# Reordering the start and the second attention batch of a two-block adaLN kernel in split fp32r

## The chip, the cores and the metric

The kernel runs on 1 NeuronCore of a Trainium2 chip. The metric is the device time in microseconds (us) of one execution, as the median of three runs. Below, PE is TensorE, DVE is VectorE, ACT is ScalarE, POOL is GpSimd, and SP is the engine whose queue issues all DMAs.

## The reference

Four batches of 512 tokens by 512 features pass through an attention-like block and then a feed-forward block, each with its own adaptive layer norm.

```python
mod = (_silu(c) @ wmod).reshape(4, 6, 1, -1)        # sa, ca, ga, sb, cb, gb
h = _layernorm(x) * (1 + ca) + sa
x = x + ga * attn(h)                                # ga, gb: sign kept, magnitude at least 0.25
h = _layernorm(x) * (1 + cb) + sb
x = x + gb * ffn(h)
...
def attn(X):
    Xn = _layernorm(X, gamma, beta)
    Q, K, V = split(Xn @ W_in + b_in)
    K, V = rotary(K), rotary(V)                     # first half of the features
    A = sum over tokens of (K/|K|) * (V/|V|)        # one row of 512 per batch
    A = 0.5 * A + 0.5
    return (A * Q) @ W_out + b_out + X
def ffn(x):
    top-2 gate, softmax summed; relu(x @ W_up.T) @ W_down.T + sum * (x @ W_expert)
```

## The kernel before, in words

**Arithmetic.** Every fp32 product is made of three fp32r products: each operand is split into a high part (ACT or POOL copies it to fp32r) and a low part (original minus high part, on DVE or POOL), and `three` (L1223) multiplies high by high, high by low and low by high. So each weight chunk of 128 rows needs a high and a low part before PE can use it. `split_hi_kv(i, k)` on ACT (L574) makes the high part of chunk k of W_K (i=0) or W_V (i=1). The low part comes from `low_kv(i, k)` on POOL (L428) or `split_lo_kv(i, k)` on DVE (L1076).

**Order.** There is no scheduler. Each engine's instructions stand in the order in which they are written, and semaphores join the engines. A wait therefore holds up everything behind it on its engine. Attention runs over the batches b = 0 to 3, then the feed-forward block over the same batches.

**The start (batch 0).** SP loads the columns, then four 256 KB chunks of the scale rows (wmod[1], into the slot of x batch 2), row tile 0 of x, four 256 KB chunks of the shift rows (wmod[0], into the slot of x batch 3), row tile 1 of x, the identity, row tiles 2 and 3, and the eight chunks of W_K and W_V in turn. PE multiplies the scale chunks (bank 2) and then the shift chunks (bank 3) in `mod_first` (L1233). For each row tile t of x, DVE takes the row's statistics (`x0_stats`, L1047), subtracts and scales (`scale_row0`, L1058), applies 1/std and the shift (`h_row0`, L1068), and takes statistics of the result. POOL raises to the power -0.5 (`rstd_x0`, `shift_h0`), ACT normalises to z, PE transposes z (`transposes0`), ACT applies gamma and beta and makes the high part (`t0_evac`), and DVE makes the low part (`t0_split`). Only then does PE start `kv_tile(0, 0)`.

**One attention batch b (`attention` on each engine, L344, L683, L973, L472).** PE runs `kv_tile(b, 0)`, the output rows of batch b-1, `kv_tile(b, 1)` to `(b, 3)`, and then four chunks of Q, with the transposes of the next batch's z between them. `transposes(b+1, 0)` waits for all four row tiles of z. `transposes(b+1, 2)` and `kv_tile(b, 3)` wait for `kv_products` on DVE, which reads the PSUM banks that they overwrite (`kv_tile(b, 3)` for those of tile 1, `transposes(b+1, 2)` for those of tile 3). Last come `a_sums`, which wait for DVE's `a_pairs`. DVE adds biases (`kv_rows`), makes rotated products (`kv_products`, L858), sums them with weights from POOL (`kv_sum`), finishes the output rows of batch b-1 (`finish_rows`, after the gates have come from DRAM in batch 1), and builds h of batch b+1: `h_row` (L808) adds the shift to what POOL's `scale_rows` (L463) scaled, and `h_stats`, `h_aggr`, POOL's `rstd_h` and DVE's `h_shift` give ACT what `normalise` needs.

**Statistics of x for the later batches.** Batch 1 takes them at the start, batch 2 between the Q splits of `attention(1)` on DVE. Batch 3 takes them in `attention(1)` too, mostly on ACT: `x_sums` and `x_squares` (L591, L599) are eight passes with accumulation, `x_mean` and `x_var` on DVE (L790, L795) finish them, POOL's `rstd_x(3)` and DVE's `x_shift(3)` follow, and ACT runs `normalise_x(3)` at the very end of `attention(1)`, ahead of `q_evac(1, 0)`.

Of the kernel before, what the change touches and what calls it, by code (L numbers as in the profile page):

```python
# [37 lines left out]
def build(nc, X, cols, ident, rot, w, wmod, brow, out):  # L38
# [14 lines left out]
    with ctx:  # L53
# [49 lines left out]
        xss = sb("xss", [P, NT])  # L103
# [13 lines left out]
        xjunk = sb("xjunk", [P, D], mybir.dt.bfloat16)  # L117
# [64 lines left out]
        xsum_s = sem("xsum_s")  # L182
        xmn_s = sem("xmn_s")
# [102 lines left out]
        def _(sp):  # L286

            sp.dma_start(col[:], cols).then_inc(col_in, 16)
            for k in range(NC):
                sp.dma_start(x_slot(2)[:, k * D:(k + 1) * D], wmod[1][:, k * D:(k + 1) * D]).then_inc(ca_w[k], 16)  # L290
            def load_x0(i):
                rows0 = X0_PARTS[i]
                sp.dma_start(x_slot(0).rearrange("p (t d) -> p t d", t=NT)[:, rows0, :],
                             x_batch[0][:, rows0, :]).then_inc(x0_in[i], 16)

            load_x0(0)
            for k in range(NC):
                sp.dma_start(x_slot(3)[:, k * D:(k + 1) * D], wmod[0][:, k * D:(k + 1) * D]).then_inc(sa_w[k], 16)
# [80 lines left out]
        def _(pool):  # L379
# [92 lines left out]
            def attention(b):  # L472
# [17 lines left out]
                else:  # L490
# [11 lines left out]
                    if b + 2 < B:  # L502
                        rstd_x(b + 2)
# [26 lines left out]
            shift_h0(1)  # L530
            rstd_x0(2)
            low_kv(0, 1)
# [3 lines left out]
            low_kv(1, 3)  # L536
# [13 lines left out]
        def _(act):  # L550
# [39 lines left out]

            def x_sums():  # L591

                act.wait_ge(x_in, (B - 1) * 16)
                for t in range(NT):
                    wait(act, xsum_s, t)
                    nc.scalar.activation(xjunk[:], xs[:, tok(B - 1, t)], ACT.Identity,
                                         accum_out=xsum[:, t:t + 1]).then_inc(xsum_s, 1)

            def x_squares():  # L599

                act.wait_ge(xmn_s, 1)
                for t in range(NT):
                    act.wait_ge(xsum_s, NT + t)
                    nc.scalar.activation(xjunk[:], xs[:, tok(B - 1, t)], ACT.Square, bias=xmn[:, t:t + 1],
                                         accum_out=xss[:, t:t + 1]).then_inc(xsum_s, 1)
# [77 lines left out]
            def attention(b):  # L683
# [20 lines left out]
                if b + 2 < B:  # L704
                    normalise_x(b + 2)
# [10 lines left out]
            split_hi_kv(0, 1)  # L716
            normalise(0, 1, 1)
            split_hi_kv(1, 1)
# [46 lines left out]
        def _(dve):  # L765
# [24 lines left out]
            def x_mean():  # L790

                dve.wait_ge(xsum_s, NT)
                v.tensor_scalar(xmn[:], xsum[:], -1.0 / D, None, ALU.mult).then_inc(xmn_s, 1)

            def x_var():  # L795
                dve.wait_ge(xsum_s, 2 * NT)
                v.tensor_scalar(xve[:], xss[:], 1.0 / D, EPS, ALU.mult, ALU.add).then_inc(xve_s, 1)

            def x_shift(g):
                dve.wait_ge(xrs_s, g + 3)  # L800
                wait(dve, xn_s, (g - 1) * NT)
                if g < B - 1:
                    v.scalar_tensor_tensor(xnm[:], xmv[:, :, 0], -1.0, xrs[:], ALU.mult, ALU.mult).then_inc(xnm_s, 1)
                else:
                    dve.wait_ge(xmn_s, 1)
                    v.tensor_tensor(xnm[:], xmn[:], xrs[:], ALU.mult).then_inc(xnm_s, 1)
# [166 lines left out]
            def attention(b):  # L973
# [16 lines left out]
                if b == 1:  # L990
                    x_mean()
                kv_sum(b, 0)
                if b < B - 1:
                    h_row(b + 1, 0)
                else:
# [23 lines left out]
                if b + 2 < B:  # L1019
                    x_shift(b + 2)  # L1020
# [55 lines left out]
            def split_lo_kv(i, k):  # L1076
                dve.wait_ge(whi_v if i else whi_k, k + 1)
                dve.wait_ge(wlo_v if i else wlo_k, k)
                v.tensor_tensor(w_lo_of(W_ORDER[i], k), w_raw[i][:, k * D:(k + 1) * D],
# [33 lines left out]
            h_row0(3)  # L1113
            t0_split(1)
# [105 lines left out]
        def _(pe):  # L1220
# [12 lines left out]
            def mod_first(bank, src, sems):  # L1233
                for k in range(NC):
                    pe.wait_ge(sems[k], 16)
                    last = mm(ps[:, bank, :], sc0[:, k, :], src[:, k * D:(k + 1) * D], start=(k == 0), stop=(k == NC - 1))
                last.then_inc(bc_ps, 1)
# [138 lines left out]
            mod_first(2, x_slot(2), ca_w)  # L1376
            mod_first(3, x_slot(3), sa_w)
# [118 lines left out]
```

## Time and profile before

| what | value |
|---|---|
| three runs | 363.78 us median (363.32 to 365.0) |
| the profiled execution | 365.14 us, of which the span of the instructions is 363.4 us |
| granted PE clock | 1.00 in every slice of the span |
| PE busy | 353.1 us, 97% of the span |
| DVE, ACT, POOL busy | 247.9, 159.1 and 126.6 us |
| DMA | 27.45 MB, most of it in the first 70 us |

The page's timeline divides the span into 40 slices of 9.1 us. PE is at 90% and more in nearly all of them, and less in the first three. DVE is at 90% and more from the fourth slice to the eighth (27 to 73 us). Idle time of PE counts one for one, since it is busy to the end; the question for any other engine is whether PE waits for it.

A matmul's own duration is modelled as longer than its share of the array: in a run of them, one starts about 0.23 us after the other and shows 0.40 us. So the idle time that is written at a stall of PE is about 0.16 us less than what the stall costs.

### The profile page before, as it was taken

What the parts mean: (1) busy time and instruction counts of PE and PEld (TensorE: products, weight loads), DVE (VectorE), ACT (ScalarE), POOL (GpSimd) and SP (SyncE); (2) the same over time, 40 slices, a digit from 0 to 9 for tenths busy, and PEclk for the clock granted to TensorE, in tenths of its full rate; (3) what the DMA queues carried; (4) which work ended last, traced back from release to release, by engine and by line L of the source; (5) the groups of instructions that cost most, each with busy time, mean ns of one, the idle gap of its engine ahead of it and who ended that gap; (6) DMA issues with size and microseconds to landing.
All of it is one profiled execution on the core that took longest, in us unless ns stands there. A gap on an engine that the chain in (4) does not pass through costs nothing.

```text
span 363.4 us, 4952 instructions
## 1 busy us (share of the span) xinstructions
PE 353.1 (97%) x1794; PEld 288.5 (79%) x1794; DVE 247.9 (68%) x508; ACT 159.1 (44%) x301; POOL 126.6 (35%) x131
## 2 busy tenths in 40 slices
PE   8799999999999999999999999999999999999996
PEld 5257587788777788888888898988988898889885
DVE  2689999979977778786977469338623852382474
ACT  1296838647169501476018753444234423441110
POOL 0395879777726166243531324800100010000000
PEclk9999999999999999999999999999999999999999
DMA  6998482370120000000000003101100110011003
GB/s 182 388 406 317 194 318 89 137 213 0 25 63 2 0 2 29 1 1 2 0 31 0 0 2 115 32 0 58 60 0 2 58 59 2 0 60 58 2 1 115
DMA packets 10985, 27.45 MB, mean 76 GB/s; under 512 B 1216, under 2 KB 1600, under 8 KB 9808
## 3 DMA queue, kind: packets, MB, share of 16 engines
q1 hardware_dynamic: 10960, 27.13, 21.1%
q8 instruction: 14, 0.23, 0.3%
q14 instruction: 11, 0.09, 0.1%
HBM read 22.90 MB, written 4.23 MB: 75 GB/s over the span
## 4 chain that ended last, share of the span: by engine, by line
PE 60%; DVE 12%; ACT 8%; issue 7%; DMA 5%; POOL 5%; SPq 2%; POOLq 0%; DVEq 0%; ACTq 0%
PE ps L1225 19%; PE ps L1227 19%; PE ps L1226 19%; PE ps L1284 2%; DMA gate_bc<-mod_rows 2%; DMA xs<-in_X 2%; POOL w_lo L414 2%; DVE hb L815 1%; DVE hst L825 1%; ACT z L626 1%; POOL hrs L411 1%; ACT ps L638 1%; DMA mod_rows<-xs 1%; ACT ps L585 1%; ACT z L617 1%
## 5 line engine op out<-in xcount | busy, mean ns | idle before, releaser
L1225 PE MATMUL ps<-wv_hi,t_hi 128*128 128x260 f32 (+1 forms) x192 | 61.7, 322 | 0.9 <-POOL wv_lo L414 0.5
L1227 PE MATMUL ps<-wv_hi,t_lo 128*128 128x260 f32 (+1 forms) x192 | 61.4, 320 | 0.0
L1226 PE MATMUL ps<-wv_lo,t_hi 128*128 128x260 f32 (+1 forms) x192 | 61.4, 320 | 0.0
L1225 PE MATMUL ps<-w_hi,g_hi 128*128 128x512 f32 (+1 forms) x132 | 51.2, 388 | 0.0
L1225 PE MATMUL ps<-t_hi,w_hi 128*128 128x512 f32 x128 | 50.6, 396 | 0.1
L1227 PE MATMUL ps<-w_hi,g_lo 128*128 128x512 f32 (+1 forms) x132 | 50.6, 383 | 0.0
L1226 PE MATMUL ps<-w_lo,g_hi 128*128 128x512 f32 (+1 forms) x132 | 50.6, 383 | 0.0
L1227 PE MATMUL ps<-t_hi,w_lo 128*128 128x512 f32 x128 | 50.0, 390 | 0.0
L1226 PE MATMUL ps<-t_lo,w_hi 128*128 128x512 f32 x128 | 49.9, 390 | 0.0
L1225 PEld LDWEIGHTS ps<-wv_hi,t_hi 128*128 128x128 f32 x192 | 36.1, 188 | 5.1 <-POOL wv_lo L414 1.4
L411 POOL TENSOR_TENSOR hrs<-hve,expo 128x4 f32<-128x4 f32 (+2 forms) x12 | 11.1, 923 | 81.9 <-DVE hve L832 62.8
L1227 PEld LDWEIGHTS ps<-wv_hi,t_lo 128*128 128x128 f32 x192 | 36.1, 188 | 2.9
L1226 PEld LDWEIGHTS ps<-wv_lo,t_hi 128*128 128x128 f32 x192 | 36.1, 188 | 2.8
L1225 PEld LDWEIGHTS ps<-w_hi,g_hi 128*128 128x128 f32 x132 | 24.8, 188 | 5.1 <-DVE g_lo L907 0.5
L1227 PEld LDWEIGHTS ps<-w_hi,g_lo 128*128 128x128 f32 x132 | 24.8, 188 | 4.9
L1226 PEld LDWEIGHTS ps<-w_lo,g_hi 128*128 128x128 f32 x132 | 24.8, 188 | 4.7
L1227 PEld LDWEIGHTS ps<-t_hi,w_lo 128*128 128x128 f32 x128 | 24.0, 188 | 5.1
L1225 PEld LDWEIGHTS ps<-t_hi,w_hi 128*128 128x128 f32 x128 | 24.1, 188 | 5.0 <-issue 0.4
L1142 DVE SCALAR_TENSOR_TENSOR g_lo<-ps,g_hi 128x512 fp32r<-128x512 f32 x16 | 11.1, 692 | 24.7 <-ACT g_hi L655 24.6
L1226 PEld LDWEIGHTS ps<-t_lo,w_hi 128*128 128x128 f32 x128 | 24.1, 188 | 4.7
L571 ACT ACTIVATE sqj<-ps 128x512 bf16<-128x512 f32 x16 | 9.5, 591 | 41.5 <-DVE ps L854 36.5
L1225 PE MATMUL ps<-w_hi,t_hi 128*128 128x512 f32 x64 | 26.1, 408 | 1.2 <-DVE prod L873 0.9
(153 smaller groups left out, 703.8 us busy)
## 6 DMA issues: line engine op xcount, KB each, us to landing
stage<-in_w SPq DMA_DIRECT2D x5, 1024.0 KB, 4.8
out<-xs SPq DMA_DIRECT2D x15, 256.0 KB, 2.0
xs<-in_X SPq DMA_DIRECT2D x3, 1024.0 KB, 9.5
xs<-in_wmod SPq DMA_DIRECT2D x8, 256.0 KB, 5.9
stage<-in_w SPq DMA_DIRECT2D x8, 256.0 KB, 8.1
xs<-in_wmod SPq DMA_DIRECT2D x2, 1024.0 KB, 7.7
gate_bc<-mod_rows SPq DMA_DIRECT2D x8, 256.0 KB, 3.9
gate_bc<-in_wmod SPq DMA_DIRECT2D x1, 1024.0 KB, 13.3
```

Source lines behind the costliest of these rows:

```text
L411: nc.gpsimd.tensor_tensor(hrs[:, t0:t0 + n], hve[:, t0:t0 + n], expo[:, 0:n], ALU.pow).then_inc(hrs_s, n)
L414: nc.gpsimd.tensor_tensor(w_lo_of(W_ORDER[i], k), w_raw[i][:, k * D:(k + 1) * D], w_hi_of(W_ORDER[i], k).bitcast(f32), ALU.subtract).then_ ...
L571: nc.scalar.activation(sqj[:], src, ACT.Square, accum_out=nsq[:, t % 2, i:i + 1]).then_inc(nsq_s, 1)
L585: nc.scalar.activation(part, part, ACT.Identity, bias=col[:, COL_BETA + c:COL_BETA + c + 1], scale=col[:, COL_GAMMA + c:COL_GAMMA + c + 1] ...
L617: nc.scalar.activation(z[:, t, :], xs[:, tok(g, t)], ACT.Identity, bias=xnm[:, t:t + 1], scale=xrs[:, t:t + 1]).then_inc(xn_s, 1)
L626: nc.scalar.activation(z[:, t, :], src, ACT.Identity, bias=hnm[:, t:t + 1], scale=hrs[:, t:t + 1]).then_inc(z_s, 1)
L638: nc.scalar.activation(whole, whole, ACT.Identity, bias=bias, scale=scale).then_inc(t_full, 1)
L1142: v.scalar_tensor_tensor(g_lo[:, c, :], ps[:, U_BANKS[c % 2], :], 0.0, g_hi[:, c, :].bitcast(f32), ALU.max, ALU.subtract).then_inc(u_los, 1)
L1225: mm(dst, l_hi, r_hi, start=start, stop=False)
L1226: mm(dst, l_hi, r_lo, start=False, stop=False)
L1227: return mm(dst, l_lo, r_hi, start=False, stop=stop)
L1284: last = nc.tensor.transpose(ps[:, t_bank(g, c), t * P:(t + 1) * P], z[:, t, c * P:(c + 1) * P], idn[:])
```

## The change

It has five parts.

1. SP loads shift chunk 0 right behind scale chunk 0, and row tile 0 of x stays behind the scales. PE multiplies in the order scale 0, shift 0, scale 1 to 3, shift 1 to 3.
2. Weight parts: POOL makes the low part of W_K chunk 1 ahead of `rstd_x0(2)`. The low part of W_V chunk 3 moves from POOL to DVE, between `h_row0(3)` and `t0_split(1)`. ACT makes the high part of W_V chunk 1 ahead of `normalise(0, 1, 1)`.
3. Statistics of x batch 3: the passes on ACT, `x_mean` and `x_var` are gone. DVE takes them with `bn_stats` between the Q splits of `attention(2)`, as batch 2's are taken in `attention(1)`. `rstd_x(3)` moves to the end of POOL's `attention(1)`, and `x_shift(3)` and `normalise_x(3)` move into `attention(2)`.
4. `h_row(b+1, 0)` moves on DVE from ahead of `kv_rows(b, 1)` to behind `kv_products(b, 1)`, in batches 1 and 2.
5. One wait in `split_lo_kv` stands twice.

```diff
             sp.dma_start(col[:], cols).then_inc(col_in, 16)
-            for k in range(NC):
-                sp.dma_start(x_slot(2)[...], wmod[1][...]).then_inc(ca_w[k], 16)
+            load_scale(0)
+            load_shift(0)
+            for k in range(1, NC):
+                load_scale(k)
             load_x0(0)
-            for k in range(NC):
-                sp.dma_start(x_slot(3)[...], wmod[0][...]).then_inc(sa_w[k], 16)
+            for k in range(1, NC):
+                load_shift(k)
             load_x0(1)
...
POOL attention(b):
                     weight(b, 1)
-                    if b + 2 < B:
-                        rstd_x(b + 2)
                     rstd_h(b + 1, 0, NT)
...
                     for t in range(NT):
                         base(b + 1, t)
+                    if b == 1:
+                        rstd_x(3)
...
POOL start:
             shift_h0(1)
+            low_kv(0, 1)
             rstd_x0(2)
-            low_kv(0, 1)
             low_kv(1, 1)
             low_kv(1, 2)
             low_kv(0, 3)
-            low_kv(1, 3)
             shift_h0(2)
...
ACT attention(b):
                 norm_sums(b, 0)
-                if b == 1:
-                    normalise_x(2)
-                    x_sums()
-                    x_squares()
+                if b < B - 1:
+                    normalise_x(b + 1)
                 norm_sums(b, 1)
...
                     t_evac(b + 1, c)
-                if b + 2 < B:
-                    normalise_x(b + 2)
...
ACT start:
             split_hi_kv(0, 1)
+            split_hi_kv(1, 1)
             normalise(0, 1, 1)
-            split_hi_kv(1, 1)
...
DVE attention(b):
                     q_split(b - 1, c)
-                    if b == 1:
-                        x_row_stats(2, c)
-                if b == 1:
-                    x_aggr(2)
+                    if b < B - 1:
+                        x_row_stats(b + 1, c)
+                if b < B - 1:
+                    x_aggr(b + 1)
                 kv_rows(b, 0)
                 kv_products(b, 0)
-                if b == 1:
-                    x_shift(2)
+                if b < B - 1:
+                    x_shift(b + 1)
...
                 finish_rows(b - 1)
-                if b == 1:
-                    x_mean()
                 kv_sum(b, 0)
-                if b < B - 1:
-                    h_row(b + 1, 0)
-                else:
+                if b == B - 1:
...
                 kv_rows(b, 1)
-                if b == 1:
-                    x_var()
                 kv_products(b, 1)
                 if b < B - 1:
+                    h_row(b + 1, 0)
                     h_row(b + 1, 1)
...
                 kv_products(b, 2)
-                if b + 2 < B:
-                    x_shift(b + 2)
                 kv_sum(b, 2)
...
DVE start:
             h_row0(3)
+            split_lo_kv(1, 3)
             t0_split(1)
...
PE start:
-            mod_first(2, x_slot(2), ca_w)
-            mod_first(3, x_slot(3), sa_w)
+            first_rows()
```

On POOL at the start, behind the second small product for the first row tile, the kernel before has this (xrs is 1/std of x's rows, hrs and hnm that of h; w_lo belongs to W_K and wv_lo to W_V):

```order
L398 TENSOR_TENSOR hnm<-xmn,hrs 128x1
L381 TENSOR_TENSOR xrs<-xve,expo 128x2
L414 TENSOR_TENSOR w_lo<-stage,w_hi 128x512
L414 TENSOR_TENSOR wv_lo<-stage,wv_hi 128x512 x2
L414 TENSOR_TENSOR w_lo<-stage,w_hi 128x512
L414 TENSOR_TENSOR wv_lo<-stage,wv_hi 128x512
L411 TENSOR_TENSOR hrs<-hve,expo 128x1
```

and the change has this:

```order
L403 TENSOR_TENSOR hnm<-xmn,hrs 128x1
L419 TENSOR_TENSOR w_lo<-stage,w_hi 128x512
L386 TENSOR_TENSOR xrs<-xve,expo 128x2
L419 TENSOR_TENSOR wv_lo<-stage,wv_hi 128x512 x2
L419 TENSOR_TENSOR w_lo<-stage,w_hi 128x512
L416 TENSOR_TENSOR hrs<-hve,expo 128x1
```

So xrs of row tiles 2 and 3 now stands behind a low part, and one low part is gone.

On DVE in `attention(1)`, from the last output row of batch 0 to the statistics of the next h, the kernel before has this (hb<-hb,sa_bc is `h_row`):

```order
L916 TENSOR_TENSOR hb<-ps,hb 128x512
L793 TENSOR_SCALAR xmn<-xsum 128x4
L882 TENSOR_SCALAR acc<-prod,wgt 128x768
L815 TENSOR_TENSOR hb<-hb,sa_bc 128x512
L854 TENSOR_TENSOR ps<-ps,bkv_bc 128x512
L856 TENSOR_TENSOR v_sb<-ps,bkv_bc 128x512
L797 TENSOR_SCALAR xve<-xss 128x4
L863 TENSOR_TENSOR cross<-ps,v_sb 128x128
...
L873 TENSOR_TENSOR prod<-ps,rot_sb 128x256
L815 TENSOR_TENSOR hb<-hb,sa_bc 128x512
L819 BN_STATS hst<-hb 128x6 x2
```

and the change has this:

```order
L887 TENSOR_TENSOR hb<-ps,hb 128x512
L853 TENSOR_SCALAR acc<-prod,wgt 128x768
L825 TENSOR_TENSOR ps<-ps,bkv_bc 128x512
L827 TENSOR_TENSOR v_sb<-ps,bkv_bc 128x512
L834 TENSOR_TENSOR cross<-ps,v_sb 128x128
...
L844 TENSOR_TENSOR prod<-ps,rot_sb 128x256
L786 TENSOR_TENSOR hb<-hb,sa_bc 128x512 x2
L790 BN_STATS hst<-hb 128x6 x2
```

Three instructions fewer stand ahead of the products of tile 1, and one more (the moved `h_row`) behind them.

## Rows read from the trace of the kernel before

**Rows 1.** The page: busy us (share of the span) and instructions of each engine.
```profile
PE 353.1 (97%) x1794; PEld 288.5 (79%) x1794; DVE 247.9 (68%) x508; ACT 159.1 (44%) x301; POOL 126.6 (35%) x131
```

**Rows 2.** Timeline, PE's stalls in batch 1: start us, us, engine line op [idle before <-releaser].
```profile
94.18 0.48 PE L1225 MATMUL ps<-w_hi,t_hi 128*128 128x512 f32 x1 [0.87 <-DVE prod L873]
...
105.93 1.09 PE L1284 MATMUL ps<-idn,z 128*128 128x128 f32 x8 [0.46 <-ACT z L626]
...
110.33 0.84 PE L1284 MATMUL ps<-idn,z 128*128 128x128 f32 x6 [0.56 <-DVE prod L873]
```

**Rows 3.** Timeline, DVE, the statistics of row tile 1 of x.
```profile
13.17 0.69 DVE L1051 BATCH_NORM_STATS2 xst<-xs 128x6 f32<-128x512 f32 x1 [2.45 <-DMA xs<-in_X]
```

**Rows 4.** Timeline, ACT and POOL, weight parts at the start.
```profile
20.67 0.62 ACT L577 ACTIVATE w_hi<-stage 128x512 fp32r<-128x512 f32 x1
```
```profile
20.56 0.71 POOL L381 TENSOR_TENSOR xrs<-xve,expo 128x2 f32<-128x2 f32 x1
21.36 1.30 POOL L414 TENSOR_TENSOR w_lo<-stage,w_hi 128x512 fp32r<-128x512 f32 x1
22.61 1.31 POOL L414 TENSOR_TENSOR wv_lo<-stage,wv_hi 128x512 fp32r<-128x512 f32 x1
```

**Rows 5.** Timeline, DVE, row tile 2 to the statistics of batch 1.
```profile
22.25 0.75 DVE L1074 SCALAR_TENSOR_TENSOR hb<-hb,xrs,ps 128x512 f32<-128x512 f32 x1
...
24.11 0.68 DVE L1079 TENSOR_TENSOR w_lo<-stage,w_hi 128x512 fp32r<-128x512 f32 x1
...
27.88 2.46 DVE L777 BATCH_NORM_STATS2 xst<-xs 128x6 f32<-128x512 f32 x4
```

**Rows 6.** Timeline, PE: start of the first row tile, W_K chunk 2, second row tile.
```profile
21.55 0.50 PE L1225 MATMUL ps<-w_hi,t_hi 128*128 128x512 f32 x1
...
24.87 0.47 PE L1225 MATMUL ps<-w_hi,t_hi 128*128 128x512 f32 x1
...
29.32 0.39 PE L1225 MATMUL ps<-w_hi,t_hi 128*128 128x512 f32 x1
```

**Rows 7.** Timeline, POOL's row scaling, and one DVE operation beside it and alone.
```profile
35.85 4.57 POOL L470 TENSOR_TENSOR hb<-z,ca_bc 128x512 f32<-128x512 f32 x3
```
```profile
37.49 1.77 DVE L815 TENSOR_TENSOR hb<-hb,sa_bc 128x512 f32<-128x512 f32 x1
...
40.38 0.68 DVE L815 TENSOR_TENSOR hb<-hb,sa_bc 128x512 f32<-128x512 f32 x1
```

**Rows 8.** Timeline, the end of batch 0 on ACT and PE.
```profile
54.77 1.52 ACT L626 ACTIVATE z<-hb,hnm,hrs 128x512 f32<-128x512 f32 x2 [5.65 <-DVE hnm L836]
```
```profile
56.59 1.03 PE L1284 MATMUL ps<-idn,z 128*128 128x128 f32 x8
```

**Rows 9.** Timeline, DVE in batch 1.
```profile
85.35 0.95 DVE L793 TENSOR_SCALAR xmn<-xsum 128x4 f32<-128x4 f32 x1
...
87.86 1.79 DVE L815 TENSOR_TENSOR hb<-hb,sa_bc 128x512 f32<-128x512 f32 x1
...
93.95 1.29 DVE L815 TENSOR_TENSOR hb<-hb,sa_bc 128x512 f32<-128x512 f32 x1
...
99.22 0.17 DVE L832 TENSOR_SCALAR hve<-hmv 128x4 f32<-128x4 f32 x1
```

**Rows 10.** Timeline, POOL in batch 1.
```profile
92.14 2.56 POOL L470 TENSOR_TENSOR hb<-z,ca_bc 128x512 f32<-128x512 f32 x2
```

**Rows 11.** Timeline, PE and DVE about the output rows of batch 1 and in batch 2.
```profile
122.27 0.39 PE L1227 MATMUL ps<-w_hi,g_lo 128*128 128x512 f32 x1
122.71 0.50 PE L1225 MATMUL ps<-w_hi,g_hi 128*128 128x512 f32 x1
```
```profile
137.43 0.70 DVE L854 TENSOR_TENSOR ps<-ps,bkv_bc 128x512 f32<-128x512 f32 x1 [2.57 <-PE ps L1227]
...
141.33 0.42 DVE L873 TENSOR_TENSOR prod<-ps,rot_sb 128x256 f32<-128x256 f32 x1
...
156.85 0.42 DVE L873 TENSOR_TENSOR prod<-ps,rot_sb 128x256 f32<-128x256 f32 x1
```

More of the change, by code:

```diff
@@ L102, in build @@
         nmu = xmn
-        xss = sb("xss", [P, NT])
         xst = sb("xst", [P, NT, 6])
@@ L116, in build @@
         sqj = sb("sqj", [P, D], mybir.dt.bfloat16)
-        xjunk = sb("xjunk", [P, D], mybir.dt.bfloat16)
         a_col = sb("a_col", [P, NC])
@@ L181, in build @@
         base_s = sem("base_s")
-        xsum_s = sem("xsum_s")
-        xmn_s = sem("xmn_s")
         kv_ps, kb_s, kv_sb = sem("kv_ps"), sem("kb_s"), sem("kv_sb")
@@ L288, in _, with load_scale, load_shift @@
             sp.dma_start(col[:], cols).then_inc(col_in, 16)
-            for k in range(NC):
+            def load_scale(k):
                 sp.dma_start(x_slot(2)[:, k * D:(k + 1) * D], wmod[1][:, k * D:(k + 1) * D]).then_inc(ca_w[k], 16)
+            def load_shift(k):
+                sp.dma_start(x_slot(3)[:, k * D:(k + 1) * D], wmod[0][:, k * D:(k + 1) * D]).then_inc(sa_w[k], 16)
             def load_x0(i):
@@ L589, in t0_evac @@
                                      ACT.Copy).then_inc(t_his, 1)
[L591 to L605, printed above, removed]
             def normalise_x1(t):
@@ L788, in x_aggr @@
                 v.tensor_scalar(xve[:], xmv[:, :, 1], EPS, None, ALU.add).then_inc(xve_s, 1)
[L790 to L797, printed above, removed]
             def x_shift(g):
@@ L801, in x_shift @@
                 wait(dve, xn_s, (g - 1) * NT)
-                if g < B - 1:
-                    v.scalar_tensor_tensor(xnm[:], xmv[:, :, 0], -1.0, xrs[:], ALU.mult, ALU.mult).then_inc(xnm_s, 1)
-                else:
-                    dve.wait_ge(xmn_s, 1)
-                    v.tensor_tensor(xnm[:], xmn[:], xrs[:], ALU.mult).then_inc(xnm_s, 1)
+                v.scalar_tensor_tensor(xnm[:], xmv[:, :, 0], -1.0, xrs[:], ALU.mult, ALU.mult).then_inc(xnm_s, 1)
             def h_row(g, t):
@@ L989, in attention @@
                 finish_rows(b - 1)
-                if b == 1:
-                    x_mean()
                 kv_sum(b, 0)
-                if b < B - 1:
-                    h_row(b + 1, 0)
-                else:
+                if b == B - 1:
                     for t in range(NT):
@@ L1078, in split_lo_kv @@
                 dve.wait_ge(wlo_v if i else wlo_k, k)
+                dve.wait_ge(wlo_v if i else wlo_k, k)
                 v.tensor_tensor(w_lo_of(W_ORDER[i], k), w_raw[i][:, k * D:(k + 1) * D],
@@ L1231, in idle_products, with first_scale, first_shift, first_rows @@
                     mm(ps[:, IDLE_BANK, 0:2 * P], acc[:, 0:P], acc[:, 0:2 * P], start=True, stop=True)
[L1233 to L1236, printed above, removed]
+            def first_scale(k):
+                pe.wait_ge(ca_w[k], 16)
+                return mm(ps[:, 2, :], sc0[:, k, :], x_slot(2)[:, k * D:(k + 1) * D], start=(k == 0), stop=(k == NC - 1))
+            def first_shift(k):
+                pe.wait_ge(sa_w[k], 16)
+                return mm(ps[:, 3, :], sc0[:, k, :], x_slot(3)[:, k * D:(k + 1) * D], start=(k == 0), stop=(k == NC - 1))
+            def first_rows():
+                first_scale(0)
+                first_shift(0)
+                for k in range(1, NC):
+                    last = first_scale(k)
+                last.then_inc(bc_ps, 1)
+                for k in range(1, NC):
+                    last = first_shift(k)
                 last.then_inc(bc_ps, 1)
```

1 line of the change is left out of this document (removed).

## The prediction

> **What bounds the kernel now.** I read the page first: PE is busy for 97% of the span [rows 1]. What a change of order can win is therefore only time in which PE waits. I then went through PE's timeline for those places. From 30 us to the end there are three of weight, all in batch 1 [rows 2]: 0.87 us on DVE's products of tile 1, 0.46 us on ACT's z, 0.56 us on DVE's products of tile 3. With the 0.16 us that a modelled end hides they cost 1.03, 0.62 and 0.72 us, 2.4 us together. A fourth is small: the last chunk of the first output row starts 0.44 us after its forerunner instead of 0.23 [rows 11], 0.2 us. Batches 2 and 3 show nothing like it. The start is the other place, since PE's first tile runs from 21.55 us to 29.32 us [rows 6], 7.8 us, although its 24 matmuls are 5.6 us of work at 0.23 us each.
>
> **Shift chunk ahead (part 1).** The bytes in front of row tile 1 of x stay the same, so it lands when it did, at 13.17 us [rows 3]. DVE takes that row's statistics (0.69 us and two short steps) before it applies the shift to row tile 0, and these end at about 14.1 us, when PE's shift product is finished in either order. I take 0 us. What hides the product is that landing and those statistics; without them PE would gain one chunk's product, some 0.4 to 0.9 us. The scale rows end one chunk later, and row tile 0 lands one chunk later; both have a microsecond or more until 13.17 us, since DVE waited 2.45 us there [rows 3].
>
> **Weight parts (part 2).** On POOL the low part of W_K chunk 1 cannot come sooner than before: its high part on ACT ends at 20.67 + 0.62 = 21.29 us, and it started at 21.36 us [rows 4]. So the change buys nothing with its first move, and xrs of row tiles 2 and 3, which filled the gap from 20.56 us, comes behind it: from 22.61 to 23.3 us. DVE's `h_row0(2)` waits for xrs and goes from 22.25 to 23.4 us, +1.15 us [rows 5]. The low part of W_K chunk 2, on DVE, stood 1.86 us behind it (24.11 us) and is now wanted at 25.25 us. There POOL is at work on W_V's chunk 2, and this decides how the move is priced. One and the same addition of two SBUF tensors on DVE took 1.77 us while POOL scaled rows, and 0.68 us alone [rows 7]: it stood still until POOL's instruction was done. By that, DVE gets its turn when POOL's chunk ends (POOL's pace is 22.61 - 21.36 = 1.25 us each, so xrs to 23.3, W_V 1 to 24.6, W_V 2 to 25.9) and ends at about 26.4 us. PE starts chunk 2 at 26.45 us instead of 24.87, +1.6 us [rows 6]. From here it has 12 matmuls to its second tile, 2.8 us, where it needed 4.45 us before because it waited for POOL's last low parts. With W_V chunk 3 on DVE that wait is short, and the second tile begins at about 29.5 us instead of 29.32: **+0.2 us**, between -0.4 (DVE is not held) and +0.6.
>
> The Trainium skill, "SBUF — State Buffer", Shared GPSIMD/Vector port, says that DVE operations with two SBUF inputs and GpSimd operations take a common port pair as an exclusive lock for the whole instruction. The 1.77 us beside 0.68 us agree. Without such a lock the moved low part would be free work on DVE, and this part would be -0.4 us instead of +0.2; the rule speaks against moving it while POOL works, and for counting each `h_row` beside POOL at twice its length or more.
>
> DVE itself comes out later than PE. It has the 1.15 us, 0.6 us for the added low part and some 0.3 us of standing still, less the near 1 us that it idled ahead of its second split: batch 1's statistics start at about 29.2 us instead of 27.88, +1.3 us [rows 5]. From there to the end of batch 0 DVE has hardly a gap (90% and more busy in each slice of the page), so the lateness is carried. PE meets it at `transposes(1, 0)`: z was done at 54.77 + 1.52 = 56.29 us and used at 56.59 us [rows 8], 0.3 us of slack. So batch 0 ends later by 1.3 - 0.3 = **+1.0 us**, which includes the 0.2 above. Bounds: -0.4 us, if POOL's turns swallow DVE's lateness, as a DVE operation that arrives late at a busy POOL loses nothing; +2.2 us, if it is held once more on each of two scalings in [rows 7].
>
> **Batch 1 (parts 3 and 4).** Taken away ahead of DVE's products of tile 1: `x_mean` 0.95 us, and `h_row(2, 0)` 1.79 us [rows 9]. These 2.7 us are more than the 1.03 us of the first stall, so **that stall goes**. The next one is another matter. `transposes(2, 0)` needs z of all rows, z needs the statistics that DVE finished at 99.22 + 0.17 = 99.39 us [rows 9], and the moved `h_row(2, 0)` now stands inside that chain. DVE can start on tile 1 when PE has done it: PE wants tile 3 at 94.18 - 1.03 = 93.15 us, tile 2 ahead of it is 24 matmuls or 5.6 us, so at 87.6 us and a little more, 87.85. Batch 2 needed from 137.43 to 141.33 + 0.42 = 141.75 us, 4.3 us, for that work [rows 11], with one operation held by POOL; without that it is about 3.5 us. So the products are done and the rows of h start at 91.3 to 92.4 us, instead of 93.95 us for the second of them [rows 9]. But POOL is in its two scalings from 92.14 us, 2.56 us [rows 10], so both first rows are held for about a scaling each, where one was held before (1.29 us). The end of the statistics comes to 98.6 us in the better order of turns and 99.7 us in the worse, against 99.39 us. I take the middle, -0.25 us. **So the first stall's 1.03 us largely comes back as a longer second one**, and of 2.4 us I count -0.25, and another -0.15 for `x_shift(3)`, which leaves the chain to the third stall. Bounds: -2.4 (all stalls go) and +0.3.
>
> **Batch 2 (parts 3 and 4).** The 0.2 us ahead of the output rows goes, since `normalise_x(3)` no longer stands ahead of ACT's Q evacuation: **-0.2 us** (0 to -0.2). DVE gets four row statistics between the Q splits; `attention(1)` does the same with batch 2's and PE doesn't wait there. `h_row(3, 0)` now stands behind the products of tile 1. The chain from 137.43 us ended at 156.85 + 0.42 = 157.27 us [rows 11], about 0.2 us before PE wanted it. One more row is 0.6 us, less what POOL, undisturbed by the row, is sooner. I take **+0.1 us**, between 0 and +0.5. Batch 3 and the feed-forward block are untouched.
>
> **Sum.** +1.0 - 0.25 - 0.15 - 0.2 + 0.1 = **+0.5 us**. The profiled execution took 365.14 us for a span of 363.4 us, 1.4 us over the median of the runs; on its own time the sum gives a span of 363.9 us and 365.6 us, on the median 363.78 + 0.5 = **364.3 us**. A measurement of this kernel tells about 0.5%, 1.8 us, from no change.
>
> **The rivals.**
> - *All of batch 1's stalls go and the start breaks even (0.17).* For it: the 2.7 us taken away exceed the 2.4 us of stalls, batch 2 runs the same instructions without them, and the turns of POOL and DVE may fall well. Against it: POOL scales batch 1's rows at 92.14 us, where batch 2's are early. 363.78 - 2.4 - 0.2 + 0.3 = 361.5 us.
> - *DVE's late start of batch 0 compounds (0.18).* Its place is `h_row0(2)`, which waits for xrs behind a low part. If DVE comes to POOL's scalings after 36 us so late that it is held once more, the lateness is 2.2 us or more at `transposes(1, 0)` and PE pays it; it decides from 2.1 us on. With the worse turns in batch 1 (+0.15) and +0.3 in batch 2: 363.78 + 2.2 + 0.15 - 0.2 + 0.3 = 366.2 us, slower.
> - *The start is swallowed (0.15).* PE's slack and POOL's turns absorb DVE's 1.3 us: 363.78 + 0 - 0.4 - 0.1 = 363.3 us.
> - *The reordered loads change when row tile 1 of x lands (0.05).* Everything up to 30 us hangs on 13.17 us, and the trace has one order only. By a chunk or more either way, about 1 us: 363.3 or 365.3 us.
>
> **How the numbers follow.** The forecast, anything within a microsecond of 364.3, has 0.45. The first rival is mostly below 361.96 (0.5% faster), the second mostly above 365.6: **0.17 faster, 0.65 same, 0.18 slower**. The range leaves out the outer half of each of the two: **362.0 to 366.2 us**.
>
> **What would show it.** In the profile after: x's row tile 1 still at about 13.2 us; DVE's row with xrs of tile 2 at about 23.4 us; PE at W_K chunk 2 near 26.4 us and at the second tile near 29.5; `transposes(1, 0)` about 1 us late with PE idle on ACT's z; no idle of PE on products of tile 1 in batch 1, but about 1.3 us ahead of `transposes(2, 0)`, on z; two long `h_row` there; nothing ahead of the output rows of batch 1; a few tenths ahead of `transposes(3, 2)`. I am wrong if PE starts chunk 2 before 25.5 us, if `transposes(1, 0)` is on time, or if the stall on z in batch 1 is gone too.

## The result, and the profile after

The changed kernel takes 365.62 us (median of 20 runs, 364.82 to 366.05), the kernel before beside it 364.46 us (20 runs, 362.38 to 365.32). The ratio is 1.0039, 95% interval 1.0029 to 1.0048: slower by 0.39% by the ratio and by 1.16 us (0.32%) by the medians, a difference that the interval bears out, and within the 0.5% that the prediction calls no change. The forecast was 364.3 us, range 362.0 to 366.2. The kernel before spreads over almost 3 us and the changed one over 1.2 us. That is a finding too: 17 of the changed kernel's 20 runs are slower than the slowest run of the kernel before.

The changed kernel's profiled execution took 364.96 us (span 363.1 us), at the low end of its runs; that of the kernel before took 365.14 us (363.4 us), at the high end of its own. Put side by side, these two profiles say "0.2 us faster".

Busy times on the page after [rows 1]:

```profile
PE 353.1 (97%) x1794; PEld 288.7 (80%) x1794; DVE 249.6 (69%) x516; ACT 153.4 (42%) x285; POOL 124.7 (34%) x130
```

PE's sum is the same. ACT has 16 instructions and 5.7 us less, which are the eight statistics passes and the reads of their sums. DVE has 8 instructions and 1.7 us more.

The statistics of x's row tile 1 started 0.76 us earlier than in the profile before [rows 3]. The six profiles with the old order of loads have this row anywhere from 12.30 to 13.50 us and the eight with the new order from 12.41 to 12.89, so one profile of each says nothing about the order. Everything below is compared by its distance from this row:

```profile
12.41 0.69 DVE L1015 BATCH_NORM_STATS2 xst<-xs 128x6 f32<-128x512 f32 x1 [0.53 <-DMA xs<-in_X]
```

Timeline after, POOL and then DVE, weight parts at the start [rows 4, 5]:

```profile
20.61 1.30 POOL L419 TENSOR_TENSOR w_lo<-stage,w_hi 128x512 fp32r<-128x512 f32 x1 [0.84 <-ACT w_hi L581]
21.86 0.72 POOL L386 TENSOR_TENSOR xrs<-xve,expo 128x2 f32<-128x2 f32 x1
22.53 2.56 POOL L419 TENSOR_TENSOR wv_lo<-stage,wv_hi 128x512 fp32r<-128x512 f32 x2
```
```profile
22.61 0.75 DVE L1038 SCALAR_TENSOR_TENSOR hb<-hb,xrs,ps 128x512 f32<-128x512 f32 x1 [1.22 <-POOL xrs L386]
...
24.47 1.17 DVE L1044 TENSOR_TENSOR w_lo<-stage,w_hi 128x512 fp32r<-128x512 f32 x1
...
28.29 2.46 DVE L761 BATCH_NORM_STATS2 xst<-xs 128x6 f32<-128x512 f32 x4
```

The chain is the one forecast: xrs behind the low part, DVE 1.22 us idle on it, and W_K chunk 2's low part held until POOL's two W_V chunks ended (25.09 us), 1.17 us where it took 0.68.

Timeline after, PE: its stalls over 0.2 us at the start and at the end of batch 0, with the first matmul of the second row tile (28.63 us) between them, then in batches 1 and 2 [rows 2, 6, 8]:

```profile
23.89 0.50 PE L1191 MATMUL ps<-wv_hi,t_hi 128*128 128x512 f32 x1 [0.30 <-POOL wv_lo L419]
...
25.69 0.50 PE L1191 MATMUL ps<-w_hi,t_hi 128*128 128x512 f32 x1 [0.84 <-DVE w_lo L1044]
...
28.63 0.39 PE L1191 MATMUL ps<-w_hi,t_hi 128*128 128x512 f32 x1
...
57.50 0.47 PE L1191 MATMUL ps<-t_hi,w_hi 128*128 128x512 f32 x1 [0.33 <-DVE prod L844]
```
```profile
105.19 1.09 PE L1262 MATMUL ps<-idn,z 128*128 128x128 f32 x8 [1.12 <-ACT z L614]
...
109.60 0.63 PE L1262 MATMUL ps<-idn,z 128*128 128x128 f32 x4 [0.57 <-DVE prod L844]
...
156.84 1.06 PE L1262 MATMUL ps<-idn,z 128*128 128x128 f32 x8 [0.31 <-DVE prod L844]
```

The stall on tile 1's products (0.87 us before) is gone; the one on z went from 0.46 to 1.12 us. The stall of 0.33 us at 57.50 us, on DVE's products at the end of batch 0, is new.

### The profile page after: what moved, and what is told of

Same layout as the page of the kernel before. It is cut to its first block, busy times and chain, and to the rows that moved or that the text cites. A ratio compares the mean times of both kernels' runs of the same rounds, so it can differ in the third digit from the quotient of the medians.

```text
span 363.1 us, 4943 instructions
## 1 busy us (share of the span) xinstructions
PE 353.1 (97%) x1794; PEld 288.7 (80%) x1794; DVE 249.6 (69%) x516; ACT 153.4 (42%) x285; POOL 124.7 (34%) x130
## 4 chain that ended last, share of the span: by engine, by line
PE 59%; DVE 16%; issue 11%; ACT 5%; POOL 5%; DMA 2%; SPq 1%; POOLq 0%; DVEq 0%
PE ps L1191 19%; PE ps L1193 18%; PE ps L1192 18%; PE ps L1262 2%; DVE hb L786 2%; DMA xs<-in_X 2%; ACT z L614 2%; POOL w_lo L419 2%; POOL hrs L416 1%; DVE hst L796 1%; DVE prod L838 1%; DVE hst L790 1%; ACT sqj L575 1%; DVE ps L842 1%; ACT z L605 1%
```

## The experiments

Twelve kernels were run in three lots of four, each beside the kernel before, the second lot on another chip than the first and third. The kernel before stood at a median of 364.55 us in the first lot, 364.48 in the second and 363.60 in the third, so kernels of different lots are compared by their ratios to it. The ratio in the table is not the quotient of the two medians: in the third lot the two differ by up to 0.0013, or 0.5 us, so a smaller difference in that lot is not to be read. The second table makes eight of the profiles comparable: the start of PE's transposes, less the start of the row on x's row tile 1 above. The places are `transposes(1, 2)` in batch 0, `transposes(2, 0)` and `transposes(2, 2)` in batch 1, and `transposes(3, 2)` in batch 2.

| kernel | median us (runs) | ratio to before, 95% interval |
|---|---|---|
| parts 1 and 2 (with 5) | 365.41 (12) | 1.0023, 1.0011 to 1.0036 |
| parts 3 and 4 | 365.03 (12) | 1.0012, 0.9999 to 1.0025 |
| part 1 | 364.34 (12) | 0.9989, 0.9974 to 1.0004 |
| part 3 | 364.15 (12) | 0.9991, 0.9976 to 1.0006 |
| before, DVE first at 57 us | 363.88 (12) | 0.9985, 0.9970 to 1.0001 |
| change, DVE first | 365.11 (12) | 1.0014, 1.0000 to 1.0028 |
| change, POOL first | 367.04 (6) | 1.0070, 1.0049 to 1.0091 |
| part 3, DVE first | 363.27 (9) | 0.9966, 0.9951 to 0.9981 |
| before, gates ahead of x | 363.37 (12) | 0.9991, 0.9976 to 1.0006 |
| change without part 4 | 363.89 (12) | 1.0001, 0.9984 to 1.0017 |
| change, W_V chunk 3 on POOL | 364.93 (12) | 1.0025, 1.0011 to 1.0039 |
| parts 1 and 3, DVE first, gates ahead | 363.44 (12) | 0.9983, 0.9969 to 0.9997 |

| distance, us | (1, 2) | (2, 0) | (2, 2) | (3, 2) |
|---|---|---|---|---|
| before | 47.52 | 92.76 | 97.16 | 144.27 |
| change | 48.00 | 92.78 | 97.19 | 144.43 |
| part 1 | 48.90 | 92.62 | 97.02 | 144.13 |
| parts 1 and 2 | 49.25 | 93.00 | 97.41 | 144.67 |
| part 3 | 47.55 | 91.08 | 94.69 | 141.82 |
| parts 3 and 4 | 47.51 | 91.99 | 96.40 | 143.84 |
| before, gates ahead of x | 47.56 | 91.30 | 95.70 | 142.81 |
| change without part 4 | 47.99 | 91.50 | 95.53 | 142.47 |

### The change cut in two, and its harmless halves

The edits are the parts as the section on the change lists them; the first kernel has parts 1, 2 and 5, the others one or two parts each.

```diff
 parts 1, 2, 5:   loads, weight parts of POOL, ACT and DVE as in the change; batches as before
 parts 3 and 4:   attention(b) as in the change; everything ahead of it as before
 part 1:          loads and PE's order of products alone
 part 3:          statistics of x batch 3 alone; h_row(b + 1, 0) where it was
```

> Only the start of the change (parts 1, 2 and 5: loads, weight parts, the doubled wait); batches 1 to 3 as before. Theory A (the prediction): DVE comes late out of the start and PE pays about +1.0 us by the end of batch 0, nothing else changes, so +0.8 to +1.2 us against before. Rival B (the start breaks even): within 0.3 us of before. In the profile A wants the start of PE's third weight chunk about 1.6 us later, counted from the landing of x's row tile 1, and transposes(1, 0) or a_sums late by 0.5 us or more.

> Only parts 3 and 4 (statistics of x batch 3 on DVE, h_row(b+1, 0) behind the products of tile 1); the start as before. Theory A: the stall on tile 1's products goes, most of it comes back ahead of transposes(2, 0), so -0.5 us against before (-0.2 to -0.9). Rival C (all stalls of batch 1 go): -2 us or more.

> Only part 1: shift chunk 0 loaded and multiplied behind scale chunk 0. Theory A: the landing of x's row tile 1 decides and is unmoved, 0 us (within 0.3 us). Rival D (the order of the loads moves that landing): as much as the landing moves, some 0.5 to 1 us either way, on the median of the rounds.

> Only part 3: statistics of x batch 3 on DVE in attention(2), h_row(2, 0) stays ahead of tile 1. Theory A: x_mean and ACT's eight passes go and h_row(2, 0) is not in the chain behind the products, so the rows of h end about 1 us sooner than in the kernel before: -1.2 us or more against before, and faster than parts 3 and 4 together by 0.5 us or more. If moving h_row(2, 0) helps instead (rival), this is slower than parts 3 and 4 together, with PE still waiting for tile 1's products.

Measured: parts 1 and 2 are at +0.86 us over the kernel before, part 1 alone at -0.21 (same), so part 2 is 365.41 - 364.34 = +1.07 us. Those two forecasts hold, though `transposes(1, 0)` with parts 1 and 2 is only 0.30 us late where 0.5 was to show. Part 3 alone is -0.40 (same) where -1.2 or more was expected, and with part 4 it is +0.48 where -0.5 was: both missed, and the second with the wrong sign. What held is that part 4 costs on top of part 3, 365.03 - 364.15 = +0.88 us. By the medians both halves of the change are losses, 0.86 + 0.48 = 1.34 against 1.16 for the whole, but for parts 3 and 4 the interval still takes in no change.

Two things did not fit. Part 3 alone was profiled at a span of 360.7 us, 362.47 us in all and the lowest of its 12 runs, without any stall in batch 1, yet its median is 364.15. And in the table part 1 has the same start as the kernel before but reaches `transposes(1, 2)` 1.4 us later. The timeline of DVE and of POOL, first of the changed kernel and then of the kernel with parts 1 and 2, shows a tie:

```profile
57.39 1.02 DVE L856 SCALAR_TENSOR_TENSOR acc<-prod,wgt,acc 128x768 f32<-128x768 f32 x1
```
```profile
57.44 2.13 POOL L411 TENSOR_TENSOR w_lo<-stage,w_hi 128x512 fp32r<-128x512 f32 x1
```
```profile
57.39 2.15 DVE L893 SCALAR_TENSOR_TENSOR acc<-prod,wgt,acc 128x768 f32<-128x768 f32 x1
```
```profile
57.43 1.29 POOL L415 TENSOR_TENSOR w_lo<-stage,w_hi 128x512 fp32r<-128x512 f32 x1
```

DVE's `kv_sum(0, 2)` and POOL's low part of the output weights' chunk 1 begin 0.04 to 0.05 us apart in all nine profiles that have no wait there. In seven DVE has its 1.02 us and POOL stands; in two, of part 1 and of parts 1 and 2, POOL has its 1.29 us and DVE stands. When POOL wins, PE stalls ahead of `transposes(1, 2)`, here in the kernel with parts 1 and 2:

```profile
61.66 1.06 PE L1312 MATMUL ps<-idn,z 128*128 128x128 f32 x8 [1.20 <-DVE prod L881]
```

That gave a theory for the spread and for part of the result, which the next lot tested.

### The tie decided by a wait

```diff
 out_weight(1) on POOL, "DVE first":
                 pool.wait_ge(whi_out, k + 1)
+                if k == 1:
+                    pool.wait_ge(kacc, 3)
 kv_sum(0, 2) on DVE, "POOL first":
                     dve.wait_ge(kacc, n)
+                    if n == 2:
+                        dve.wait_ge(wlo_out, 2)
```

> The kernel before, with one wait added: GpSimd's low part of the output weights' second chunk waits for VectorE's kv_sum(0, 2). Both are wanted within 0.05 us of each other at 57.7 us in batch 0, and whichever comes first holds the other for about 1.1 us. Tie theory: in the profile kv_sum(0, 2) takes 1.02 us always, batch 1 shows the stall of about 0.9 on tile 1's products and 0.5 on z as in the kernel before, and the times of this kernel spread less than those of the kernel before beside it (under 1.5 us instead of 2 to 3), round 364 to 365. Rival (the spread comes from the loads' landing at the start, not from the tie): it spreads as the kernel before does, 2 to 3 us.

> The changed kernel, with the same added wait, so that VectorE always has kv_sum(0, 2) first. Tie theory: its profiled execution had that outcome and stood at 364.96 us where its runs have a median of 365.62; so with the outcome fixed the median falls to 364.9 or so (364.5 to 365.2), and the changed kernel is no slower than the kernel before with the same wait by more than 0.3 us. Rival (the changed kernel's own steps cost 1 us, the tie nothing): 365.5 as without the wait, and 1 us above the kernel before with the wait.

> The changed kernel, with the opposite wait: kv_sum(0, 2) waits for the second low part of the output weights, so that GpSimd is always first. Tie theory: VectorE's row of kv_sum(0, 2) ends 1.1 us later (58.7 + 1.0), TensorE stalls 1.1 to 1.2 us ahead of transposes(1, 2), the stall of 1.12 us ahead of transposes(2, 0) shrinks by as much or goes, and the median is 365.6 to 366.1, 0.7 to 1.2 us over the changed kernel with VectorE first. Rival (what TensorE loses in batch 0 it gets back whole in batch 1): both within 0.3 us.

> Part 3 of the change alone (x's variance root and GpSimd's place for it moved), with the wait that gives VectorE kv_sum(0, 2) first. In the earlier profile of part 3 alone with that outcome TensorE had no stall in batch 1 and the span was 360.7 us, 2.6 under the kernel before, while the median of its runs was only 0.3 under. Tie theory: with the outcome fixed all runs are like that profile: 362.4 to 362.9, 1.5 to 2 us under both kernels. Rival (360.7 was one lucky landing of the loads or of the gates): 364.1 as without the wait, with its profile at 363.

Measured: the kernel before with DVE first still spreads from 363.14 to 365.96 us. **The tie theory falls as the cause of the spread.** The rival's sign, an unchanged spread, is there; its cause, the landing of the loads at the start, is not shown by this run. The change with DVE first has 365.11 us, still 365.11 - 363.88 = 1.23 us over the kernel before with the same wait (about 1.1 by the ratios), so the rival is right: the change's own steps cost over 1 us without the tie. With POOL first the median is 367.04 us, 1.9 over the one with DVE first instead of the forecast 0.7 to 1.2. That median stands between two groups. Three of the six runs show a mean granted PE clock of 0.994 to 0.995 and took 367.8 to 368.1 us. The other three, at 0.998 to 1.00 like all twelve with DVE first, took 366.0 to 366.3 us, which is 0.9 to 1.2 us over the median of these. Beside that, this kernel overdoes its case: DVE waits for the semaphore and starts at 59.26 us, so PE's stall is 2.08 us where the tie, lost by itself, made 1.20:

```profile
59.26 1.02 DVE L858 SCALAR_TENSOR_TENSOR acc<-prod,wgt,acc 128x768 f32<-128x768 f32 x1 [1.52 <-POOL w_lo L411]
```

Part 3 with DVE first is 363.27 us, under the kernel before by 0.34% (0.19 to 0.49), and again no stall over 0.2 us in batch 1. It missed the forecast 362.4 to 362.9, and its rival's 364.1 as well, but it is the fastest of the study by ratio. Against the kernel before with the same wait it is 363.88 - 363.27 = 0.61 us faster.

The kernel before with DVE first showed what I had missed. Its profile has a span of 361.4 us, and the stall on tile 1's products is not there. The timeline of DVE of the kernel before, and then of the same with DVE first, at the first output rows of batch 0:

```profile
79.51 1.29 DVE L916 TENSOR_TENSOR hb<-ps,hb 128x512 f32<-128x512 f32 x2 [1.46 <-DMA gate_bc<-mod_rows]
```
```profile
77.57 1.29 DVE L918 TENSOR_TENSOR hb<-ps,hb 128x512 f32<-128x512 f32 x2
```

In the profile that the prediction rests on, DVE stood 1.46 us for the gates' broadcasts. In the other it did not stand for them. The DMA queue of the kernel before shows 1 MB of x queued 0.1 us behind them:

```profile
70.67 1.76 SPq L359 DMA_DIRECT2D gate_bc<-mod_rows  x4
72.54 0.38 SPq L313 DMA_DIRECT2D xs<-in_X  x1
```

### The gates, part 4, one edit of part 2, and a kernel from the pieces

```diff
 before, gates ahead of x:
             sp.wait_ge(modt_ps, 1)
+            sp.wait_ge(ga_in, B * 16)
             load_x(3)
 change without part 4:
+                if b < B - 1:
+                    h_row(b + 1, 0)
...
                 kv_products(b, 1)
                 if b < B - 1:
-                    h_row(b + 1, 0)
                     h_row(b + 1, 1)
 change, W_V chunk 3 on POOL:
+            low_kv(1, 3)
             shift_h0(2)
...
             h_row0(3)
-            split_lo_kv(1, 3)
             t0_split(1)
```

> The kernel before, where the load of x's last batch (1 MB, issued 0.1 us behind the four broadcasts of the gates) waits until these have landed. In the kernel before the fourth broadcast landed at 79.49 us, 3.6 behind the third, and VectorE stood 1.46 us for it at 78.05; in the same kernel with VectorE first at the tie it landed at 77.54 and there was neither that idle time nor the stall of 0.87 on tile 1's products. Gate theory (the load takes the broadcasts' bandwidth, and how much is chance): the fourth lands within 1.5 us of the third (76.0 to 77.0), VectorE doesn't stand for it, TensorE's stall at 94 us goes, and the median is 363.5 to 363.9, 0.6 to 1.0 under the kernel before. Rival (the stall on the products has another cause and the gates' landing is a bystander): 364.5 as before, the stall still there.

> The changed kernel without part 4: h_row(b+1, 0) back ahead of the second tile's products. Theory (part 4 brings the stall on z, since it makes VectorE's h_row take 3.0 us beside GpSimd's rows and end the second batch's statistics 2 us later; part 3 alone had hve at 96.4 and no stall in batch 1): the stalls ahead of transposes(2, 0) (1.12), of kv's next tile (0.57) and in batch 2 (0.31) go, and the median is 364.0 to 364.4, 1.2 to 1.6 under the changed kernel. Rival (the lateness that part 2 gives VectorE, 1.2 us from the statistics of batch 1 on, brings them): most of them stay, 365.2 or more.

> The changed kernel with one edit of part 2 undone: the low part of W_V's chunk 3 back on GpSimd, so VectorE's queue at the start is as before. In the changed kernel VectorE's w_lo was held 1.17 us there and the first statistics of batch 1 came 1.17 us later than before, measured from the landing of x's row tile 1; TensorE stalled 0.84 ahead of W_K's chunk 2 on it. Theory A (that lateness is what part 2 costs): the stall of 0.84 goes, statistics at the old distance (15.1 us behind the landing), 0.7 to 1.1 under the changed kernel: 364.5 to 364.9. Rival (the other two edits of part 2, or GpSimd's longer queue, cost as much): 365.3 or more.

> What the runs point to, put together: the kernel before with parts 1 and 3 of the change, the wait that gives VectorE kv_sum(0, 2) first, and x's last batch loaded behind the gates; parts 2 and 4 left out. Part 3 with the first wait stood at 363.27, ratio 0.9966 to the kernel before, with no stall in batch 1. Theory (part 3 has given VectorE enough slack that the gates' landing no longer matters, and part 1 is worth nothing or 0.2): 363.0 to 363.3. Rival (what the gates cost and what part 1 brings adds up): 362.2 to 362.7.

**The gates.** In the profile of the kernel before with the gates ahead the stall at 94 us is gone and DVE doesn't stand. The load of x is issued at 75.72 us, when the broadcasts have landed, and DVE's row comes without idle time. The DMA queue, and then DVE, of this kernel:

```profile
70.27 1.76 SPq L359 DMA_DIRECT2D gate_bc<-mod_rows  x4
75.72 0.38 SPq L313 DMA_DIRECT2D xs<-in_X  x1
```
```profile
77.55 1.27 DVE L917 TENSOR_TENSOR hb<-ps,hb 128x512 f32<-128x512 f32 x2
```

It reaches `transposes(2, 0)` at 91.30 instead of 92.76. The mechanism shows in this pair of profiles, its worth in the median does not: 363.37 against 363.60 us, ratio 0.9991 with an interval that takes in 1, where 0.6 to 1.0 us were expected. In this lot the kernel before itself had 20 of 35 runs under 363.9 us, against 11 of 35 in the first lot, and 10 of 12 with the gates ahead. So the gates' landing is one source of its spread, with some 1.5 us at stake in the profiles. How often it comes late in the runs without a profile isn't shown. The landing of the first loads is another source: in the six profiles with the old order PE reaches `transposes(1, 0)` 43.41 to 43.53 us behind the row of x, whether this stands at 12.30 or at 13.50 us.

**Part 4.** Without it the change has a ratio of 1.0001 instead of 1.0039, 1.4 us less, as forecast (1.2 to 1.6). By the medians over the kernel before beside each it is 1.16 - 0.29 = 0.9 us less, so its worth lies between 0.9 and 1.4 us. The stall on z is gone although the gates were late here too (DVE stood 0.60 us for them), and so are the one in batch 2 and half of the 0.57. DVE's statistics and ACT's z without part 4:

```profile
97.11 0.17 DVE L803 TENSOR_SCALAR hve<-hmv 128x4 f32<-128x4 f32 x1
```
```profile
99.44 1.52 ACT L614 ACTIVATE z<-hb,hnm,hrs 128x512 f32<-128x512 f32 x2 [9.37 <-DVE hnm L807]
```

and with it:

```profile
98.48 0.17 DVE L803 TENSOR_SCALAR hve<-hmv 128x4 f32<-128x4 f32 x1
```
```profile
100.81 1.53 ACT L614 ACTIVATE z<-hb,hnm,hrs 128x512 f32<-128x512 f32 x2 [11.01 <-DVE hnm L807]
```

1.37 us later on DVE, though the row on x's row tile 1 came 0.28 us sooner.

The stall on z that part 4 brings follows the gates' landing. In the five profiles with part 4, how long DVE stood for the gates, and PE's stall ahead of `transposes(2, 0)`:

| kernel | DVE on the gates, us | PE on z, us |
|---|---|---|
| change | 0.86 | 1.12 |
| parts 3 and 4 | 0.54 | 0.82 |
| change, DVE first | 0.34 | 0.61 |
| change, W_V chunk 3 on POOL | 0 | 0.31 |
| change, POOL first | 0 | 0.31 |

In the first four the stall is 0.26 to 0.31 us more than what DVE stood; the last had PE 2 us late already. With part 3 and without part 4 there is no such stall for 0, 0.32 and 0.60 us of standing. So part 4 costs about 0.3 us there with the gates in time, and what they are late comes on top.

**W_V chunk 3 back on POOL.** The stall of 0.84 stays (0.86 us), against the theory: it does not come from the added instruction, which stands behind it. DVE's row with xrs still waits 1.21 us for POOL here, so xrs behind the low part fits as its cause. The statistics of batch 1 come 15.27 us behind the row of x (27.78 - 12.51), against 15.88 in the change and 14.71 before (not the 15.1 of the expectation), so the added instruction has about half of DVE's lateness. PE itself is later for the undone edit, at `transposes(1, 0)` 44.07 us behind the row of x instead of 43.71. What it is worth in time stays open. By ratio the kernel is 0.5 us under the change, with intervals that overlap; by the medians it is 364.93 - 363.60 = 1.33 us over the kernel before, and the change 1.16. Its profile differs from the change's in more than the edit: the gates landed in time, POOL's two scalings came 0.7 us sooner, DVE reached its pair of `h_row` 0.55 us later, and the pair was held less. POOL and DVE of this kernel, then of the change:

```profile
90.22 2.60 POOL L475 TENSOR_TENSOR hb<-z,ca_bc 128x512 f32<-128x512 f32 x2
```
```profile
92.05 1.92 DVE L787 TENSOR_TENSOR hb<-hb,sa_bc 128x512 f32<-128x512 f32 x2
```
```profile
90.92 3.04 POOL L475 TENSOR_TENSOR hb<-z,ca_bc 128x512 f32<-128x512 f32 x2
```
```profile
91.50 3.01 DVE L786 TENSOR_TENSOR hb<-hb,sa_bc 128x512 f32<-128x512 f32 x2
```

**The pieces together.** Ratio 0.9983 (0.9969 to 0.9997), better than the change and barely better than the kernel before (0.16 us by the medians), not better than part 3 with DVE first (0.9966, 0.9951 to 0.9981); these two can't be told apart. Putting the gates ahead adds nothing that can be seen. The theory's reason, that part 3 has taken `x_mean` (0.95 us) and `x_var` from DVE there, fits the profiles of part 3, which bore 0.32 and 0.60 us of standing without a stall, but it isn't shown by this run alone. It keeps a stall of 0.54 us on DVE's products of tile 3.

## Why the prediction was right, and where its steps failed

The range and the call of "same" held. Against its own profile the sum even held to a few hundredths: +0.5 us forecast, and the span less the row of x went from 363.4 - 13.17 = 350.23 to 363.1 - 12.41 = 350.69 us, +0.46. That closeness is luck. Only +0.16 of it is there at `transposes(3, 2)`; terms that were too high and too low cancel up to there, and half of the +0.46 comes behind DVE's last instruction, where nothing was forecast. The medians say +1.16, more than twice the forecast. Step by step:

- *Shift chunk ahead*, 0 us: right. In the profile of part 1 alone PE reaches `transposes(1, 0)` 43.42 us behind the row of x, as before, and the median is 0.2 us lower, which can't be told from nothing.
- *Weight parts*, the chain at the start: right in its steps. With 0.76 us added for the landing, DVE's row with xrs is at 23.37 us (forecast 23.4), PE's chunk 2 at 26.45 (26.45), the second tile at 29.39 (29.5), the statistics at 29.05 (29.2).
- *Weight parts*, "so the lateness is carried" and batch 0 later by 1.0 us: **this step failed** in the profile. DVE's lateness of 1.17 us was cut to 0.76 at the first `h_row`, which ran at 37.49 us by the clock of both profiles. It then grew, to 1.59 us ahead of the third and fourth `h_row`, since POOL's low parts, sooner by the clock, now held a DVE operation that they had not met before (1.29 us instead of 0.29). The pair itself took it down to 0.49. DVE, before and then after:

```profile
48.15 3.48 DVE L815 TENSOR_TENSOR hb<-hb,sa_bc 128x512 f32<-128x512 f32 x2
```
```profile
48.98 2.38 DVE L786 TENSOR_TENSOR hb<-hb,sa_bc 128x512 f32<-128x512 f32 x2
```

  `transposes(1, 0)` came 0.29 us late with no idle time on z, close to the prediction's own sign of being wrong, and `transposes(1, 2)` 0.48. So +0.48 us stands where +1.0 was forecast. The bound had named the reason: what arrives late at a busy POOL loses nothing. In medians part 2 is +1.07 us; the two profiles that show it with the tie fallen alike, parts 1 and 2 against part 1, have +0.54 at `transposes(3, 2)` and +0.51 at PE's last instruction. By their spans it is +0.88, so another 0.37 us comes behind PE's end; that this is part 2's work is not shown.
- *Batch 1*, the first stall goes and comes back ahead of `transposes(2, 0)`: right, 1.12 us for a forecast of 1.3, with two `h_row` held for POOL's two scalings (3.01 us for two). For the forecast -0.25 the same profile has -0.46 (48.00 to 92.78, against 47.52 to 92.76). The -0.15 for `x_shift(3)` did not come: from `transposes(2, 0)` to `(2, 2)` both kernels need 4.4 us, and the third stall is 0.57 us for 0.56.
- But **the base of that step was wrong**, and this is why the whole is +1.16 and not +0.5. Of the stalls that it traded against each other, the 0.87 us was not every execution's: it stands in the one profile of the kernel where DVE stood 1.46 us for the gates, and in neither that has them in time, with DVE first and with the gates ahead. With the gates ahead, the kernel before is at `transposes(2, 0)` 1.46 us sooner. I had read the stall's releaser on PE and priced what DVE does ahead of it, but had not followed DVE back to its own idle 1.46 us on a DMA. So part 4 was booked as returning a gain, when with the gates in time there is less gain to return and its stall on z is a plain loss: +0.88 us on part 3, 0.9 to 1.4 us on the whole change.
- *Batch 2*, -0.2 and +0.1: from `transposes(2, 2)` to `transposes(3, 2)` the change needs 47.24 us against 47.11, +0.13 for -0.1. The 0.2 ahead of the output rows went (the chunk starts 0.22 us after its forerunner instead of 0.44), so the moved row cost about 0.35 us where 0.1 was forecast. The stall forecast at `transposes(3, 2)` is there, 0.31 us.

From `transposes(3, 2)` to the end another 0.3 us is lost between the two profiles. PE's last matmul starts 202.53 us behind it before and 202.60 after, so 0.07 us is PE's. The rest comes behind DVE's last instruction, from whose end to the end of the span it is 2.23 us before and 2.46 after. Over all fourteen profiles, which have the same code from batch 3 on, PE's part is 202.48 to 202.61 us and the whole 205.87 to 206.26, so nothing there is shown to be the change's.

Of the rivals, "all of batch 1's stalls go" has its place in part 3 alone: 94.69 - 91.08 = 3.61 us from `transposes(2, 0)` to `transposes(2, 2)`, no stall between, a span of 360.7 us. Part 4 and not the mechanism kept it away. "DVE's lateness compounds" did not happen in the profile: its lateness went to 1.59 us, under the 2.1 from which that rival decides, and then down, by the same POOL turns that broke my own step.

## What to carry to other kernels

Before a stall is traded for another, follow its releaser back until an engine that has no idle time of its own; where the chain ends at a DMA, look at other executions of the same kernel first, since the landing may be that execution's alone. And when one profile is all there is, see where its time lies among the runs: here the profile before came from the top of its runs and the one after from the bottom of its own. An instruction that goes from a place with slack to the head of the next chain is paid there: the moved `h_row`, 0.68 us by itself, made DVE's statistics 1.37 us later beside a busy POOL.

## What the runs showed of the hardware

- The order at a tie is not fixed. DVE's 128x768 addition and POOL's 128x512 subtraction, begun 0.04 to 0.05 us apart and with DVE's row first each time, took 1.02 and 2.13 us in seven of nine profiles and 2.15 and 1.29 in two. The Trainium skill, "SBUF — State Buffer", Reading the diagram, says that whichever starts first gets the shared pair for the whole instruction. That one of them stands for the whole of the other agrees with the 2.15 us; that the first to start wins is not borne out at this distance, where the row that starts first by the profile lost in those two.
- Lateness of DVE does not stay what it is beside a busy POOL: 1.17 us became 0.76, then 1.59 where one of its operations met a low part on POOL, then 0.49 behind a pair that took 2.38 us instead of 3.48. Likewise a pair of DVE instructions took 1.92 us instead of 3.01 where POOL came 0.7 us sooner and DVE 0.55 us later.
- Four broadcasts of 256 KB each, issued from 70.67 us with a load of 1 MB queued 0.1 us behind, had the last landing at 79.5 us, 8.8 us after the first issue, and DVE waited for it; in six of the eleven other profiles with that order DVE did not wait. With the load held back all four had landed 5.3 and 5.5 us after the first issue (two profiles).
- The landing of the same first loads in the same order moved by 1.2 us between executions (12.30 to 13.50 us in six profiles on two chips), and PE's `transposes(1, 0)` with it, 43.41 to 43.53 us behind.
